# First feed-forward net of an AdaLN block: the first two weight tiles' products in one interleaved stream, their operands in whole pieces

## The reference

```python
x = x + L0_ffn(L0_cond(x))      # gate/up/down with LoRA, then a net with w * (su @ sv) weights
x = x + L1_ffn(L1_cond(x))      # linear with LoRA, then an int4 net
# L0_ffn:
a = x @ (gate_w * (gate_su @ gate_sv)).T     # (1024, 512) x (512, 1792)
b = x @ (up_w * (up_su @ up_sv)).T
d = silu(a) * b
y = d @ (down_w * (down_su @ down_sv)).T
```

## Time and profile before

| | |
|---|---|
| median of 3 runs | 612.41 us (612.2 to 612.71) |
| the profiled execution | 612.5 us, of which the span from the first to the last instruction 610.9 us |
| PE busy | 601.5 us, 98% of the span |
| DVE, ACT, POOL busy | 477.9, 294.5, 300.0 us |
| share of the ending chain | PE 89%, DVE 5%, DMA 2%, others 4% |

### The profile page before, as it was taken

How to read it: one execution, slowest core, us unless ns; L and a number is a source line. 1 busy time by engine, 2 the same in 40 slices (tenths; PEclk the granted TensorE clock), 3 DMA queues, 4 the chain that set the end, 5 groups by cost and what they waited for, 6 DMA issues and landing times.

```text
span 610.9 us, 8097 instructions
## 1 busy us (share of the span) xinstructions
PE 601.5 (98%) x2904; PEld 490.8 (80%) x2904; DVE 477.9 (78%) x581; ACT 294.5 (48%) x415; POOL 300.0 (49%) x227
## 2 busy tenths in 40 slices
PE   8999999999999899999999999999999999999997
PEld 6777887878778688888888888888788888888886
DVE  6799847867768989775258888645879998999987
ACT  5754314323443444542023454333657886478860
POOL 5647234424434025851044486520004889958897
PEclk9999999999999999999999999999999999999999
DMA  7895481541171202402120200152222221322203
GB/s 252 209 229 170 146 181 48 147 112 45 53 199 43 70 18 96 154 1 91 39 70 35 70 30 31 54 96 70 82 83 89 68 72 51 105 69 70 75 13 137
DMA packets 29771, 56.06 MB, mean 92 GB/s; under 512 B 10148, under 2 KB 13764, under 8 KB 29348
## 3 DMA queue, kind: packets, MB, share of 16 engines
q1 hardware_dynamic: 27908, 52.70, 29.7%
q0 software_dynamic: 1536, 2.33, 1.6%
q10 hardware_dynamic: 288, 0.52, 0.2%
HBM read 48.44 MB, written 6.06 MB: 89 GB/s over the span
## 4 chain that ended last, share of the span: by engine, by line
PE 89%; DVE 5%; DMA 2%; issue 1%; POOL 1%; ACT 1%; SPq 0%; POOLq 0%; DVEq 0%
PE ps_down L2337 6%; PE ps_down L2338 6%; PE ps_down L2339 6%; PE ps_gate L2611 3%; PE ps_gate L2610 3%; PE ps_up L2610 3%; PE ps_up L2611 3%; PE ps_m L2610 3%; PE ps_m L2611 3%; PE ps_down L2611 3%; PE ps_down L2610 3%; PE ps_gate L2445 3%; PE ps_gate L2447 3%; PE ps_gate L2446 3%; PE ps_up L2445 2%; PE ps_up L2446 2%
## 5 line engine op out<-in xcount | busy, mean ns | idle before, releaser
L1145 POOL TENSOR_TENSOR up_sum<-up_sum,up_more 128x1024 f32<-128x1024 f32 x14 | 33.7, 2408 | 62.0 <-DVE up_more L1913 62.0
L1104 POOL TENSOR_TENSOR act_lo<-up,act_hi 128x512 fp32r<-128x512 f32 x14 | 18.1, 1295 | 70.7 <-ACT act_hi L1461 70.7
L2337 PE MATMUL ps_down<-act_hi,w_hi 128*128 128x512 f32 x112 | 43.9, 392 | 0.0
L2338 PE MATMUL ps_down<-act_lo,w_hi 128*128 128x512 f32 x112 | 43.6, 390 | 0.0
L2339 PE MATMUL ps_down<-act_hi,w_lo 128*128 128x512 f32 x112 | 43.6, 389 | 0.0
L1913 DVE SCALAR_TENSOR_TENSOR gate_sum<-ps_up,s_group,gate_sum 128x1024 f32<-128x1024 f32 x28 | 35.8, 1280 | 3.8 <-PE ps_up L2611 3.7
L1677 DVE TENSOR_TENSOR w_lo<-w_total,w_hi 128x512 fp32r<-128x512 f32 (+1 forms) x28 | 28.2, 1010 | 13.3 <-ACT w_hi L1455 12.9
L1030 POOL TENSOR_TENSOR cond_total<-w_raw 128x512 f32<-128x512 f32 x8 | 11.2, 1396 | 55.3 <-PE ps_m L2347 21.7
L1157 POOL TENSOR_TENSOR act_lo<-gate_sum,act_hi 128x1024 fp32r<-128x1024 f32 x14 | 33.7, 2416 | 6.4 <-DVE gate_sum L1921 6.4
L2445 PE MATMUL ps_gate<-x_hi,w_hi 128*128 128x512 f32 x80 | 32.1, 401 | 2.9 <-ACT m_copy L1441 1.6
L1455 ACT ACTIVATE w_hi<-w_total 128x512 fp32r<-128x512 f32 (+1 forms) x28 | 20.5, 738 | 27.8 <-POOL w_total L1098 19.3
(11 more groups left out here) (411 smaller groups left out, 2060.4 us busy)
## 6 DMA issues: line engine op xcount, KB each, us to landing
w_int<-in_ffn_gu SPq DMA_DIRECT2D x14, 512.0 KB, 3.5
w_raw<-in_ffn_gu SPq DMA_DIRECT2D x10, 512.0 KB, 4.0
w_raw<-in_cond_gu SPq DMA_DIRECT2D x9, 512.0 KB, 5.9
w_raw<-in_ffn_dn SPq DMA_DIRECT2D x8, 448.0 KB, 3.1
w_int<-in_ffn_dn SPq DMA_DIRECT2D x8, 448.0 KB, 3.2
b_rows<-b_split SPq DMA_DIRECT2D x12, 256.0 KB, 5.0
xp<-in_x SPq DMA_DIRECT2D x8, 256.0 KB, 5.0
w_raw_third<-in_ffn_gu SPq DMA_DIRECT2D x4, 512.0 KB, 3.6
```

Of the source, the lines that this page charges most:

```text
L1145: nc.gpsimd.tensor_tensor(up_sum[:, u % 3, :], up_sum[:, u % 3, :], up_more[:, u % 2, :], ALU.add).then_inc(up_done, 1)
L2337: nc.tensor.matmul(ps[:, :], weights_hi[:, cols], rhs_hi(k), start=start and n == 0, stop=False)
L2338: nc.tensor.matmul(ps[:, :], weights_hi[:, cols], rhs_lo(k), start=False, stop=False)
```

## The change

PE: the fourteen products of tiles 0 and 1 become one stream in the order of `first_order`, with `pair_scales` part 0 before 0/3 and part 1 before 1/1. The bank of each product and its waits for banks stay.

The diff, cut to its core:

```diff
-        def seven_order(q):
-            return (2, 6, 4, 3, 1, 5, 7) if q == 0 else (2, 3, 1, 4, 5, 6, 7)
+        seven_order = (2, 3, 1, 4, 5, 6, 7)
+        first_order = ((0, 2), (0, 6), (1, 2), (0, 4), (1, 4), (0, 3), (0, 1), (0, 5), (0, 7), (1, 3), (1, 1), (1, 5), (1, 6), (1, 7))
...
-        x_pieces = ((2, None), (4, None), (6, None), (3, 0), (1, 0), (5, 0), (3, 1), (1, 1), (5, 1), (7, 0), (7, 1))
+        x_pieces, x_sums = (2, 4, 6, 3, 1, 5, 7), (4, 6, 3, 1, 7)
...
POOL:
+            def third_tile_sums(ph):
+                raw, low = raw_weights(ph, 2), w7_total[0]
+                pool.wait_ge(w_summed, 7)
+                nc.gpsimd.tensor_tensor(low[:, 12 * P:14 * P], raw[:, 4 * P:6 * P], raw[:, 6 * P:8 * P], ALU.add).then_inc(w_summed, 1)
+                nc.gpsimd.tensor_tensor(low[:, 8 * P:12 * P], raw[:, 0:4 * P], raw[:, 4 * P:8 * P], ALU.subtract).then_inc(w_summed, 1)
...
ACT:
-            for n, k in x_pieces[1:6]:
-                x_high(n, k)
+            for n in (4, 6):
+                x_high(n)
             m2_to_sbuf(0)
-            for n, k in x_pieces[6:]:
-                x_high(n, k)
+            x_high(3)
+            m2_to_sbuf(1)
+            for n in (1, 5):
+                x_high(n)
+            for j in range(2):
+                act.wait_ge(seven_done, seven_count(j, 4))
+                nc.scalar.activation(gate0[j][:, :], seven_banks[j][2][:, :], ACT.Silu).then_inc(gate0_silu, 1)
+            x_high(7)
...
DVE:
+            def first_two_tiles(ph):
+                raw, total = raw_weights(ph, 2), w7_total[0]
+                seven_part(ph, 0)
+                seven_gate1(ph, 0)
+                pair_product(ph, 2, 0)
+                seven_rest(ph, 0)
+                seven_diff(ph, 1)
+                pair_product(ph, 2, 1, range(1))
...
+                seven_up0(ph, 0)
+                seven_part(ph, 1)
+                seven_rest(ph, 1)
+                for piece in range(2):
+                    piece_lo(ph, 2, piece)
+                seven_products(ph, 0)
+                pair_product(ph, 2, 1, range(1, 2))
+                piece_lo(ph, 2, 2)
+                seven_diff(ph, 2)
+                seven_gate1(ph, 1)
+                seven_up0(ph, 1)
...
PE:
+            def first_two_tiles(ph):
+                pe.wait_ge(w_prod, 2)
+                for j, n in first_order:
+                    if (j, n) == (0, 3):
+                        pair_scales(ph, 2, 0)
+                    if (j, n) == (1, 1):
+                        pair_scales(ph, 2, 1)
+                    seven_product(ph, j, n)
```

## The result

The changed kernel takes 608.95 us (median of 9 runs, 608.09 to 610.67) against 612.20 for the kernel before (9 runs, 610.59 to 612.95). The ratio is 0.9944, 95% interval 0.9933 to 0.9956: 3.4 us less, 2.7 to 4.1. The profiled execution has a span of 607.3 us instead of 610.9.

A forecast was written before the change was run, and what follows sets the result against it. PE bounds the kernel, with three stops worth 3.74 us; less 0.10 at 0/5 and 0.32 at 1/6, 3.32 is saved, taken as 3.3, from the median 612.41 to 609.1 us. Range 608.5 to 610.5.

The forecast's parts named there:

- three stops: PE's waits at 0/4, 0/3's second half and 0/5: 3.41 us plus 0.33 of restarts, 3.74 us in all.
- restart: First matmul behind each PE stop lasts 0.50 us instead of 0.39: 0.11 us per stop.
- 0/5: After the change, PE's product 0/5 and its operand diff arrive about even: 0.1 us lost, between nothing and 0.3.
- stop 1: PE waits 1.78 us at 0/4 for ACT's copy of bank c, queued behind operands that waited for DVE.
- The new wait at 1/6: PE waits at 1/6 for part_sum, behind three DVE instructions after diff: 0.21 + 0.11 = 0.32 us lost.
- x_low(7) whole: DVE's x_low(7) as one 128x1024 instruction: 1.22 us, bounds 1.2 and 2.01; at 2.01, 0/7 loses about 0.5 us.
- Tile 2's weights and POOL: Weight pieces and the two sums moved to POOL stay hidden: 0 lost at 2/2, or 0.7 us if DVE is slowed.
- Later: Everything after tile 1's end at 220.97 us starts 3.3 us sooner; the gain reaches the end undiminished.
- Rival 1: DVE sets the pace; POOL's sums holding it 2.03 us would leave 2.1 us saved, 610.3 us; 14%.
- stops 1 and 2: PE's waits of 1.78 us at 0/4 and 0.83 at 0/3's second half, both forecast gone with 0.6 us to spare.
- Rival 2: Gain given back at late operands in DVE's chain and ACT's queue: 611.2 to 613.6 us, say 612; 7%.
- Rival 3: Slower: POOL's moved sums come late, so 2/5 and the rest of tile 2 stand; 613.6 us or more; 3%.

The follow-up runs named there:

- experiment 7: Changed kernel with part_sum of tile 1 ahead of up0 of tile 0 and x_sum(7) ahead of x_low(1) on DVE: 608.50 us, ratio 0.9939 to the kernel before.
- Experiment 1: Kernel before, with only ACT's copy of bank c of tile 0 moved ahead of all half pieces: 612.39 us, ratio 1.0009.
- experiment 4: Changed kernel with all three weight sums of tile 2 on DVE, none on POOL: 609.72 us, ratio 0.9962 to the kernel before.
- experiment 6: Changed kernel with part_sum of tile 1 one place earlier on DVE, ahead of up0 of tile 0: 608.10 us, ratio 0.9931 to the kernel before.
- experiment 8: Changed kernel with both of POOL's weight sums for tile 2 made twice: 610.02 us, ratio 0.9966 to the kernel before.

## Why the prediction was right

**The stops and what removed them.** The forecast was 609.1 us, 3.3 less than before; measured were 608.95 and 3.4. The prediction took the bound to be PE's three stops, counted from start to start. Both held: the stage lost 3.30 us in the trace, and tile 2's first matmul came 20.66 us after 0/2's where 20.67 was written down. The mechanism is the forecast one, but that the figures agree to 0.01 is luck. By experiment 7 the stops were worth 3.89 us, not 3.74, in part because a restart was priced by its first matmul alone; and what is left at 0/5 and 1/6 costs 0.58 (20.65 - 20.07), not 0.42. The two shortfalls, 0.15 and 0.16, cancel. The prediction read stop 1 as ACT's copy queued behind operands that wait for DVE. Experiment 1 sharpens that: without the operands sooner or other work for PE, the early copy gives nothing. The prediction's sum did not need that distinction, since the change does all three at once; a reader who had priced the copy alone at 1.8 us would have been wrong by all of it.

**The new wait at 1/6.** Forecast 0.32 us with its restart, measured 0.32 + 0.11 = 0.43. The place, the cause (three instructions between diff and part_sum) and what removes it are shown by experiments 4 and 6. The term was sized 0.1 short, 0.07 of it in the signal from PE to DVE: that was taken at 0.04 us, and the last matmul of 1/3 is through at 214.52 (214.13 + 0.39) while diff starts at 214.63.

**0/5.** Taken at 0.1 us, between 0 and 0.3; it is the restart, 0.11 by the first matmul and 0.13 by the product.

**x_low(7) whole.** Taken at 1.22 us, bounds 1.2 and 2.01; it lasts 1.22.

**Tile 2's weights and POOL.** Taken as hidden, with 0.7 us as the other end. Piece 1 ended at 219.93, 0.8 before 2/2; the moved sums took the 2.03 us that were put for them. Piece 2 was hit, which the prediction left out: DVE's part of it, put at 1.2 us or less, took 1.74 beside POOL's next instruction. It ended at 223.39 (221.65 + 1.74); 2/5 starts four products of 1.36 us after 220.75, at 226.19, so 2.8 us were left. By the lock that the Trainium skill describes (SBUF — State Buffer, section "SBUF: two separate sides") piece 0, begun at 218.48, would wait for POOL's end at 218.78 and end at 219.46; it ended at 219.32. In experiment 8 it would have piece 1 end at 220.55 (219.87 + 0.68; 220.43 measured). So the trace agrees to 0.14 us each time, as in the earlier trace rows, with DVE the quicker.

**Later.** The gain arrived whole: 386.55 us behind the stage against 386.6.

**Rivals.** Rival 1, DVE as the pace, is half right as a reading of the kernel before: experiment 1 shows that stops 1 and 2 followed DVE's chain of operands. What it priced, POOL's sums holding DVE for 2.03 us, did not come, since up, part_sum and rest beside them kept their length. Its warning that little is to spare holds: DVE is busy for 20.03 of the 20.66 us. In experiment 4, 0.94 us more on DVE cost the stage 0.98; in experiment 8, two more sums on POOL made two DVE instructions 1.64 us longer in all and held PE for 0.71 and a restart. Rival 2 did not come: no operand was late by more than the restart at 0/5. Rival 3 did not come: POOL's larger sum ended at 218.78, 5.5 us before it would have bitten.

## What to carry to other kernels

When a wait on the busiest engine ends with some signal, ask what the next instruction behind it waits for: if that comes at the same late time, taking the first wait away moves it and wins nothing. Where a chain on another engine sets the pace for a while, a cure is work of the busy engine that needs nothing of this chain, put between; here two products and a pack, 3.2 us, were worth 2.8, against 0.5 for a shorter chain. Once the stage is nearly full, the order of single instructions on the second engine counts, here 0.42 and 0.15 us: what a waiting product needs goes ahead of what nobody waits for.

## What the runs showed of the hardware

A signal that comes just in time still costs the restart: at 0/5 the first matmul lasted 0.50 us although it started on time, the next followed 0.34 instead of 0.23 us later, and the product took 1.49 instead of 1.36. The trace shows what is lost. Each matmul has its weight load (PEld); the load of this matmul, in the changed kernel and in experiment 7:

```profile
210.15 0.19 PEld L2451 LDWEIGHTS ps_gate<-x_hi,w_hi 128*128 128x128 f32 x1 [0.27 <-DVE diff L2064]
209.95 0.19 PEld L2451 LDWEIGHTS ps_gate<-x_hi,w_hi 128*128 128x128 f32 x1
```

With the signal just in time, the load starts with its matmul, at 210.15. In experiment 7, where the signal came earlier, it starts 0.22 us ahead of its matmul (210.17) and is hidden behind the one before. At stops 1 to 3 the load starts with the matmul too (204.83, 207.87 and 210.88), so in these traces what holds a matmul holds its weight load as well.

In these traces POOL's sums lengthened DVE's instructions only where those read SBUF alone (0.68 to 1.23 and 1.77 us in experiment 8), and were lengthened by them (0.74 to 1.06, 1.29 to 1.74); instructions with an operand in PSUM kept 0.68 to 0.69 us beside them.
